# Recurrent block's norm parameters for each of the first four units by itself, and all five engines' written orders rewritten

## The reference, cut to what matters

```python
x = x + 0.5 * quantized_ffn(layernorm(x))            # q_*
x = x + recurrent_block(layernorm(x))                # f_*, m_*
x = x + 0.5 * quantized_ffn(layernorm(x))            # q_* again
x = x + 0.5 * expert_ffn(layernorm(x))               # r_*, e_*, x_*  (pass 0)
x = x + attention_with_state(layernorm(x))           # g_*
x = x + 0.5 * expert_ffn(layernorm(x))               # r_*, e_*, x_*  (pass 1)
```

## Time and profile before

| | us |
|---|---|
| median of 3 runs | 714.58 (710.06 to 716.77) |
| profiled execution, device time | 718.42 |
| its span, first to last instruction | 716.6 |
| PE busy in it | 622.6 |
| DVE, ACT, POOL busy | 483.6, 399.3, 391.5 |

### The profile page before, as it was taken

How to read it: one execution, slowest core, us unless ns; L and a number is a source line. 1 busy time by engine, 2 the same in 40 slices (tenths; PEclk the granted TensorE clock), 3 DMA queues, 4 the chain that set the end, 5 groups by cost and what they waited for, 6 DMA issues and landing times. The chain is left out here.

```text
span 716.6 us, 14593 instructions
## 1 busy us (share of the span) xinstructions
PE 622.6 (87%) x4232; PEld 486.7 (68%) x4232; DVE 483.6 (67%) x1730; ACT 399.3 (56%) x1037; POOL 391.5 (55%) x416
## 2 busy tenths in 40 slices
PE   2477999998989999898996989999999999988971
PEld 1234556565646778786886777778878988766861
DVE  6877678868899857636434886988864784545334
ACT  2387888897784545544442737264657345543530
POOL 4333552537455687776752625363567564766543
PEclk9997999999999999999998999999999999999996
DMA  7997000000031356567768030133224635566796
GB/s 265 411 409 314 1 0 1 1 0 31 16 97 45 91 160 177 171 170 219 211 190 296 31 103 9 24 100 87 68 86 138 169 117 155 156 177 192 209 321 215
DMA packets 60126, 100.99 MB, mean 141 GB/s; under 512 B 10288, under 2 KB 28592, under 8 KB 59792
## 3 DMA queue, kind: packets, MB, share of 16 engines
q1 hardware_dynamic: 50832, 81.52, 37.1%
q0 software_dynamic: 8640, 17.84, 7.0%
q10 hardware_dynamic: 576, 0.69, 0.3%
HBM read 61.79 MB, written 38.23 MB: 140 GB/s over the span
## 5 line engine op out<-in xcount | busy, mean ns | idle before, releaser
L830 POOL DMA_INDIRECT rows_by_expert<-xx,sidx x128 | 127.9, 999 | 76.5 <-DVE xx L809 41.6
L1071 PE MATMUL bank<-tint,twt 128*128 128x128 f32 x1136 | 151.6, 279 | 16.5 <-DVE thidt L1109 7.9
L1071 PEld LDWEIGHTS bank<-tint,twt 128*128 128x128 f32 x1136 | 138.5, 193 | 29.4 <-issue 14.6
L1109 DVE TENSOR_TENSOR thidt<-tsil,bank 128x256 f32<-128x256 f32 x142 | 58.6, 419 | 101.0 <-ACT tsil L1087 91.2
L1120 POOL DMA_INDIRECT rows_done<-tout,tin x98 | 94.8, 967 | 51.2 <-issue 25.5
L1087 ACT ACTIVATE tsil<-bank 128x256 f32<-128x256 f32 x142 | 53.9, 383 | 89.8 <-PE bank L1071 88.0
L1048 PE MATMUL bank<-e_dn,thidt 128*128 x568 | 89.3, 283 | 6.6 <-issue 2.6
L1048 PEld LDWEIGHTS bank<-e_dn,thidt 128*128 128x128 f32 x568 | 77.2, 194 | 19.2 <-issue 19.0
L1095 ACT ACTIVATE tout<-bank,tin 128x128 f32<-128x128 f32 x142 | 51.6, 367 | 45.6 <-PE bank L1054 43.7
L1120 POOL DMA_INDIRECT rows_done<-tout,tdst x44 | 45.1, 1026 | 54.9 <-issue 21.1
L1080 ACT ACTIVATE tint<-bank 128x128 f32<-128x128 f32 x142 | 38.7, 275 | 44.7 <-PE bank L1054 41.7
(11 more groups left out here) (270 smaller groups left out, 1340.5 us busy)
## 6 DMA issues: line engine op xcount, KB each, us to landing
twt<-moe_gu SPq DMA_DIRECT2D x142, 256.0 KB
rows_by_expert<-tout SPq DMA_DIRECT2D x25, 715.0 KB, 20.0
tin<-rows_by_expert SPq DMA_DIRECT2D x142, 65.0 KB, 2.8
hid<-rows_done SPq DMA_DIRECT2D x12, 512.0 KB, 5.8
x<-x_in SPq DMA_DIRECT2D x8, 256.0 KB, 4.4
rows_by_expert<-xx,sidx POOLq DMA_INDIRECT x128
out<-x SPq DMA_DIRECT2D x8, 256.0 KB
rows_done<-tout,tin POOLq DMA_INDIRECT x98, 2.5
```

The source lines that it names most:

```text
L830: pool.indirect_dma_start(out=rows_by_expert, out_offset=bass.IndirectOffsetOnAxis(ap=sidx[h][:, k:k + 1], axis=0), in_=xx[h][:, r, t, :], ...
L1071: m = pe.matmul(bank[UP_BANKS[p][j]][:, c * P:(c + 1) * P], weights[:, c * P:(c + 1) * P], tint[g % TURNS][:, :], start=True, stop=True)
L1109: dve.tensor_tensor(thidt[g % TURNS][:, :, :].rearrange("p j c -> p (j c)"), tsil[g % TURNS][:, :], bank[UP_BANKS[p][j]][:, INNER:2 * INNE ...
```

## The change

The recurrent block's norm parameters are made in parts: units 0, 1, 2 and 3 each by itself (`SOLO = 4`), units 4 and 5 and units 6 and 7 in pairs as before. DVE's `f_mom` and POOL's `f_root` and `f_rstd` so become six steps each in place of four; the single ones work on 128x4 tiles. The semaphores count parts. Nothing else is added or removed: every other step of the five engines is there before and after. But all five written orders are rewritten from end to end, with hundreds of steps moved by a few places.

```diff
+        def units_root(pool, ln, of):
             return to_power(pool, ln["rstd"][:, of, :], ln["ve"][:, of, :])
...
+        def units_shift(pool, ln, of, scale):
+
+            many = of.stop - of.start
             pool_step(pool, pool.tensor_tensor(ln["shift"][:, of, :], ln["msum"][:, of, :],
-                                               neg_half[:, :].rearrange("p (u t) -> p u t", u=2), ALU.mult))
+                                               neg_half[:, 0:many * TILES].rearrange("p (u t) -> p u t", u=many), ALU.mult))
...
+        SOLO = 4
+        F_PARTS = [slice(u, u + 1) for u in range(SOLO)] + [slice(u, u + 2) for u in range(SOLO, UNITS, 2)]
+
+        def f_part(u):
+
+            return 1 + next(k for k, of in enumerate(F_PARTS) if of.start <= u < of.stop)
+
+        def f_mom_vector(dve, k):
+            of = F_PARTS[k]
+            ln_moments(dve, lf, of, s_fve)
             dve.tensor_scalar(ms[:, of, :], lf["var"][:, of, :], 1.0 + RMS_EPS, RMS_EPS * LN_EPS, ALU.mult, ALU.add).then_inc(s_fve, 1)
 
-        def f_root_gpsimd(pool, i):
-            of = slice(2 * i, 2 * i + 2)
-            pool.wait_ge(s_fve, 2 * pair(i))
+        def f_root_gpsimd(pool, k):
+            of = F_PARTS[k]
+            pool.wait_ge(s_fve, 2 * (k + 1))
             pool_step(pool, to_power(pool, r1[:, of, :], ms[:, of, :]))
-            ln_shift(pool, lf, i, r1).then_inc(s_fr1, 1)
...
+            units_shift(pool, lf, of, r1).then_inc(s_fr1, 1)
+
+        def f_rstd_gpsimd(pool, k):
+            pool.wait_ge(s_fve, 2 * (k + 1))
+            units_root(pool, lf, F_PARTS[k]).then_inc(s_frstd, 1)
...
-            act.wait_ge(s_fr1, pair(u // 2))
+            act.wait_ge(s_fr1, f_part(u))
...
-            dve.wait_ge(s_frstd, pair(u // 2))
+            dve.wait_ge(s_frstd, f_part(u))
```

More of the change, by code:

```diff
@@ new lines, in _ @@
+            for j in range(26, 28):
+                t_load_sync(sp_, 0, j)
+            t_weights_sync(sp_, 0, 27)
+            for j in range(28, 31):
+                t_load_sync(sp_, 0, j)
+            t_weights_sync(sp_, 0, 28)
+            t_load_sync(sp_, 0, 31)
+            for j in range(29, 31):
+                t_weights_sync(sp_, 0, j)
+            t_load_sync(sp_, 0, 32)
+            for j in range(31, 33):
+                t_weights_sync(sp_, 0, j)
+            t_load_sync(sp_, 0, 33)
@@ L2055, in _ @@
+            for j in range(37, 39):
+                x_hid_vector(dve, 0, j)
             table_vector(dve, 0, 4)
@@ new lines, in _ @@
+            x_dst_vector(dve, 1, 60)
+            e_add_vector(dve, 7, 1)
+            x_dst_vector(dve, 1, 61)
+            x_hid_vector(dve, 1, 60)
+            for j in range(62, 64):
+                x_dst_vector(dve, 1, j)
+            x_hid_vector(dve, 1, 61)
+            x_dst_vector(dve, 1, 64)
+            x_hid_vector(dve, 1, 62)
+            x_dst_vector(dve, 1, 65)
+            x_hid_vector(dve, 1, 63)
+            x_dst_vector(dve, 1, 66)
+            x_hid_vector(dve, 1, 64)
+            c_add_vector(dve, 0, 1)
@@ L3579, in _ @@
[L3579 to L3591 removed]
+            for j in range(29, 31):
+                x_silu_scalar(act, 0, j)
@@ new lines, in _ @@
+            x_in_scalar(act, 0, 33)
+            x_silu_scalar(act, 0, 31)
+            for j in range(28, 30):
+                x_out_scalar(act, 0, j)
+            x_in_scalar(act, 0, 34)
+            x_silu_scalar(act, 0, 32)
+            e_silu_scalar(act, 6, 0, 0)
+            for j in range(33, 35):
+                x_silu_scalar(act, 0, j)
+            x_in_scalar(act, 0, 35)
+            for j in range(30, 32):
+                x_out_scalar(act, 0, j)
+            x_in_scalar(act, 0, 36)
@@ L3675, in _ @@
+            x_out_scalar(act, 0, 59)
+            x_in_scalar(act, 0, 65)
+            x_out_scalar(act, 0, 60)
+            x_in_scalar(act, 0, 66)
+            for j in range(62, 64):
+                x_silu_scalar(act, 0, j)
+            x_out_scalar(act, 0, 61)
             g_apply_scalar(act, 0)
@@ new lines, in _ @@
+            g_cross_scalar(act, 6)
+            x_silu_scalar(act, 1, 22)
+            x_in_scalar(act, 1, 23)
+            for j in range(18, 20):
+                x_out_scalar(act, 1, j)
+            x_in_scalar(act, 1, 24)
+            g_read_scalar(act, 6)
+            x_silu_scalar(act, 1, 23)
+            g_cross_scalar(act, 7)
+            x_silu_scalar(act, 1, 24)
+            x_out_scalar(act, 1, 20)
+            x_in_scalar(act, 1, 25)
+            x_out_scalar(act, 1, 21)
+            g_read_scalar(act, 7)
```

2647 lines of the change are left out of this document (1305 added, 1342 removed).

## The result

| | before | changed |
|---|---|---|
| median, us (16 runs each) | 713.71 (710.06 to 718.41) | 708.19 (701.71 to 712.06) |
| profiled execution, us | 718.42 | 704.28 |
| its span | 716.6 | 702.5 |
| PE busy in the span | 622.6 | 620.4 |

Ratio 0.9884, 95% interval 0.9859 to 0.9908: faster by 5.5 us taken from the medians, 8.3 from the ratio. I had said 710.1, in a range from 702.5 to 718.5, and gave "within 1%" the larger chance; by the ratio it is faster by 1.16% (0.92 to 1.41).

What follows compares the result with a forecast made beforehand. PE's work was taken as the bound, with only its idle time to win. Head -3.5, joint and middle 0, tail -1 summed to -4.5 us, from the 714.58 us median to 710.1, range 702.5 to 718.5.

Steps and rivals of the forecast that it cites:

- What bounds the kernel: Whole kernel: PE's 622.6 us of work is the bound; an order can win at most 94 us of idle time.
- Units 0 and 1: Start of the kernel: `f_norm` 0 starts at 25.4 against 27.55, 2.2 us earlier, masks on ACT covered by 0.2 us.
- Units 2 and 3: Before 60 us: `f_norm` 2 at 51.4, 5.1 us earlier; `f_mix` 0 at 55.7, 3.4 us earlier.
- the higher clock that I allowed for: At `f_xb` 2 (4.86 us at clock 0.50): a shorter wait keeping the higher level would give some 1.3 us.
- The head's 3.5 us: Before 60 us: norms gain 2.2 and 5.1, mixing chain 2 to 3.4; taken as 3.5 us, ends 1 and 6.
- The joint: Between the two passes, near 383 us: weights of three tiles queue behind fetches; 0 us, ends -1 and +3.
- the 5 us that I had named: Sign at the joint: PE's longest idle there stays under 5 us.
- Rival C: Slower through the joint: PE idles 5.5 us, later work delayed, together +6.4; 720.4 us in all; chance 0.13.
- The tail: Behind 680 us: row loads ahead of the fetches gain, stores behind the last fetch cost 0.5; -1 us, -2.5 to +1.9.
- The middle: 120 to 680 us apart from the joint: unknown, taken as zero, bounded by +-4 us.
- The test that I named: 120 to 680 us: the prediction falls if PE's idleness there moves by more than 4 us.
- A: Rival, everything comes through: head 5.1, tail 2.5, middle 2 us less idleness; -9.6, 705 us; chance 0.25.

Runs made afterwards that it cites:

- g1: The changed kernel itself, run again on another chip beside partial versions, against the kernel before (716.2 us): 0.986.
- g4: Kernel before, orders and pairs kept, with only ACT's `k_masks` moved ahead of `f_norm` 0, against the kernel before (716.2 us): 1.0018.
- i2: Pairs and old orders up to the joint of the passes (about 345 us), new orders behind it, against the kernel before (715.7 us): 0.9977.
- g2: Old orders throughout, with only the norm parameters of units 0 to 3 made singly, against the kernel before (716.2 us): 0.9977.
- e5: Old orders throughout, norm parameters of units 0 to 3 made singly, on a slower chip, against the kernel before (822.2 us): 0.9952.
- i1: Single parameters and new orders up to DVE's `q_out` 4 (about 60 us), old orders behind, against the kernel before (715.7 us): 0.9953.
- g3: Single parameters and new orders up to the joint (about 345 us), old orders behind, against the kernel before (716.2 us): 0.9884.
- h2: Single parameters, old orders for the first 60 us, new from there to the joint, old behind, against the kernel before (829.4 us): 0.9999.
- e8: Pairs and old orders up to DVE's `x_hid` 1, 45 (about 625 us), new orders behind, against the kernel before (822.2 us): 0.9992.
- h4: The changed kernel with old orders from DVE's `x_hid` 1, 45 (about 625 us) on, against the kernel before (829.4 us): 0.9973.
- e7: Pairs and old orders up to the joint (about 345 us), new orders behind, against the kernel before (822.2 us): 1.0108.

## Why the prediction came out as it did

**What bounds the kernel.** Held in the main. To PE's end g1 is 11.5 us ahead of before, 9.3 by idle time and 2.2 by busy time. The latter is less than what two kernels with the same work differ by (622.6 in before, 625.6 in g4). Of the waits that the prediction named, 14.5 us for `tt` became 3.1, but only 4.4 of these 11.4 us left PE's idle time before 60 us; the rest is idle time ahead of other steps now.

**Units 0 and 1.** `f_norm` 0 by sum at 25.4, measured 24.97; the masks' end at 25.2, measured 24.69, so their cover was 0.28 us on POOL's side, where I had 0.2. g4, with the masks moved alone, measured no change, with a wider cover.

**Units 2 and 3.** `f_norm` 2 said 51.4, measured 49.63: ACT does ahead of it what the sum has, from `q_copy` 3 at 44.79 on with two table loads, only 1.8 us sooner. `f_turn` 2 near 53, measured 53.32, but that is luck: the sum had it right behind the norm and left out that it waits for the bank of `f_yb` 0, which stands behind `f_norm` 2 on ACT. By the sum's own times (51.4 + 1.65 for the norm, 1.28 for the table load, 0.6) that wait ends only at 54.9. The norm came 1.8 us sooner, and `f_turn` 2 started 2.0 us behind the norm's end (49.63 + 1.64) for this wait, so the two cancel. `f_mix` 0, said 55.7, came at 54.20. Of the higher clock that I allowed for: 0.50 is granted from 52 to 56 us, and 0.89 over the first 60 us where it was 0.95, but `f_xb` 2 took 3.65 us (4.86 in the earlier trace rows), at 1.00. That gain is not the order's alone, as it took 4.36 in g1 and, with the old orders, 3.72 in i2.

**The head's 3.5 us.** Right in size: split and new head alone gave 0.9953 of 715.7, -3.4 us (-1.4 to -5.4 by its interval). How much of it is the split's and how much the new order's, the runs do not part (g2 0.9977, e5 0.9952). It came right with errors inside it, `f_turn` 2 above and this one. The shift at 54.96, 1.51 us beside DVE's scan, I took as a property of the kernel. In five of seven executions of that place it took 0.30. The exclusion of the Trainium skill (SBUF — State Buffer, Who interferes with whom), which the prediction weighed, fits the 1.51: in both executions POOL ended 0.07 us behind DVE's second product with two inputs in SBUF. Which of the two an execution draws, the traces do not show beforehand: in all seven POOL starts the step 0.15 or 0.16 us ahead of DVE's first product. Against the mean of the seven old heads (87.05 us) the add of unit 0 comes 2.5 (i1) to 3.8 us (first trace of the change) earlier, not the 4.3 to 5.6 that before's trace gives.

**The joint.** Within its ends of -1 and +3. The first trace has 4.0 us of idleness in place of 3.86; PE's longest wait there is 4.25 us in g1 and 4.93 in i2 (both new there), 3.27 in i1 and 4.16 in g2 (old) and 4.46 in g3 (old, behind new ones), all under the 5 us that I had named. Rival C, with 5.5 us and 4.8 more behind it, fell: of its mechanism about a microsecond is to be seen.

**The tail.** Said -1. Everything behind the joint together measured -1.6 us (i2) and -2.3 us (the medians of g3 and g1, with overlapping intervals), which the noise does not part from -1. The mechanism did not come as said. PE's longest wait for rows `tin` behind the last attention add fell (2.1 to 2.6 us in before, i1 and g3; 0.8 to 1.3 in the change's two traces and i2), but all its waits for them together did not: 3.3, 2.6 and 2.1 us against 2.6, 2.9 and 2.5. The 3.2 to 3.5 us of idle time that PE loses there went at the gate's product `thidt` (6.0 us on both lines in g3, 3.8 in g1) and at waits of 0.9 and 0.7 us (L958, L308) that are gone from this stretch. Behind PE's end the changed kernel gives back 1.0 us: g1 needs 15.4 us from there to the end of its span, g3 14.4. From the last fetch to the end it is 0.4 us more, where I took 0.5.

**The middle: the step that failed.** "For the other 500 us: unknown, zero." The new orders between 60 us and the joint gave 0.9884 against 0.9953, about 4.9 us (2 to 8, an estimate from the two intervals), where the sum had nothing. The bound I had put on it was 4 us either way for 560 us. The test that I named, that PE's idleness of 120 to 680 us would move by more than 4 us, did not show it: it moved by 2.5 us (39.4 to 36.9). That was a poor test, for two reasons. Its stretch lumps the middle, which gains, with the attention block, which loses: between landmarks the first trace of the change has 3.5 us less idle time from 60 us to the first add than before (18.1 for 21.6) and 1.8 more from there to the last attention add (11.5 for 9.7). And idle time is only half of the 4.1 us that the stretch lost from i1 to g3. With +0 replaced by -4.9 the sum is -3.5 - 4.9 - 1 = -9.4 us, or 0.987: the case that I called A, for which I had a chance of 0.25, and in its size (-9.6) close. But A had the head at 5.1 and 2 us for the middle; by the middle values it is the other way round, though the intervals leave open which of the two is larger.

What stays open: which moves of the middle earn and by what mechanism, since at the cut of h2 the new middle needs the new head and 248 of DVE's 639 places differ between i1 and g3; that i1 and g3 ran in different groups, each beside its own before; whether the end's order by itself is worth anything (e8 says no, 0.9992, on a chip on which little can be told; h4 can't say); and why e7 lost 1% once and, in two repetitions on other chips, nothing.

## What to carry to other kernels

A step may be worth almost nothing alone (the split, 0.9977) and still be the condition of a good order (the orders without it: 1.0101); ask of a split what may now stand behind it. The effect of a rewritten order is not zero because one can't follow it: the long full stretch, in which only one wait of PE was over 3 us, gave about as much as the head with its two of 7. A wait that is gone is not yet time won: of 11.4 us at two waits, 4.4 left the idle time. Before putting a step right behind what it waited for, read all its waits in the kernel: `f_turn` 2 had a second one. And divide the time at landmarks where the orders change, and build on no wait of about 1 us before another execution has shown it.

## What the runs showed of the hardware that I had not expected

One instruction of 128x8 elements on POOL took 1.51 us in two executions and 0.30 in five, with nearly the same orders around it and starts between 53.80 and 55.12 us. In all seven it starts 0.15 or 0.16 us ahead of the same DVE product, so the starts do not tell the two apart. The landmark 34 us behind it stands at 0 and -0.9 us in the two and at -2.0 to -2.9 in the five, a part of which is the earlier start of some.

The same program took 713.7 to 716.2 us on three occasions and 822 to 829 on three others, two of them (827.9 and 829.4) on the same chip. PE's busy time in the first 60 us was the same, 28.3 and 28.5 us in e8 and i2. Behind 120 us PE's waits of many kinds were longer, the largest row being one that the profile puts down to "issue", in e8

```profile
PE bank L1084 <- issue: 19.6, 10, 9.4
```

where before had 6.7 us in 5 waits, the longest 3.9; others are 10.4 us for `egate` (1.9 in before) and 9.9 for `tint` (0.9). PE's busy time behind 120 us was 573.0 us in place of 536.0, and the mean granted clock of before's runs 0.93 in place of 0.98. Why is open. An order's worth measured on the one need not be that on the other: the orders behind the joint were 1.0108 and 0.9995 on the two slower chips and 0.9977 on the chip of group 5, while those up to the joint, 0.9908 and 0.9884, agree within their intervals.

A table load took 1.28 us wherever it stood (37 in before's trace and 37 in the change's), as in the earlier trace rows, and ACT went on right behind it (g2, ACT):

```profile
50.78 1.28 ACT L560 ACT_TABLE_LOAD   x1
52.07 0.60 ACT L560 ACTIVATE bufC<-bank 128x512 f32<-128x512 f32 x1
```
